# Value products of a quad of heads as one series, in the wave of its former second half

## The reference

```python
q = _split_heads(hidden_states @ q_w.T + q_b)      # hidden_states = layernorm(x), 128 rows
k = _split_heads(context @ k_w.T + k_b)            # context: 12544 rows
v = _split_heads(context @ v_w.T + v_b)
scores = jnp.einsum('bhqd,bhkd->bhqk', q, k) / jnp.sqrt(jnp.float32(HD))
scores = jnp.where(mask, -jnp.inf, scores)
probs = jax.nn.softmax(scores, axis=-1)
ctx = jnp.einsum('bhqk,bhkd->bhqd', probs, v)
x = x + ctx                                        # layers 2 and 3: ctx @ wo + bo
```

## Time and profile before

| | us |
|---|---|
| median of 3 runs | 2428.49 (2421.33 to 2435.22) |
| the profiled execution | 2424.6 |
| its span, first to last instruction | 2422.8 |
| PE busy in the span | 2268.4 |
| DVE busy | 1584.7 |
| ACT busy | 1504.9 |
| granted TensorE clock, mean | 0.958 of full |

### The profile page before, as it was taken

How to read it: one execution, slowest core, us unless ns; L and a number is a source line. 1 busy time by engine, 2 the same in 40 slices (tenths; PEclk the granted TensorE clock), 3 DMA queues, 4 the chain that set the end, 5 groups by cost and what they waited for, 6 DMA issues and landing times. The chain is left out here.

```text
span 2422.8 us, 68489 instructions
## 1 busy us (share of the span) xinstructions
PE 2268.4 (94%) x26863; PEld 1892.1 (78%) x26863; DVE 1584.7 (65%) x3621; ACT 1504.9 (62%) x3044; POOL 413.6 (17%) x353
## 2 busy tenths in 40 slices
PE   7999999988999999999877999999967999999968
PEld 6888888777788788787755888888856888888758
DVE  4777777635777777777653777777735777777532
ACT  2666666634788788887523666666633666666611
POOL 3211222002221221220002122222003222212000
PEclk7999999998999999999888999999988999999969
DMA  6677666475444344341155766666517666776345
GB/s 131 116 126 126 118 115 122 61 222 149 100 118 125 99 123 115 104 119 40 46 179 117 123 107 116 116 116 117 77 52 144 121 121 121 124 125 112 49 132 173
DMA packets 152460, 279.62 MB, mean 115 GB/s; under 512 B 32829, under 2 KB 72078, under 8 KB 152218
## 3 DMA queue, kind: packets, MB, share of 16 engines
q1 hardware_dynamic: 148842, 272.18, 54.5%
q10 hardware_dynamic: 3376, 4.03, 0.7%
HBM read 120.94 MB, written 0.33 MB: 50 GB/s over the span
## 5 line engine op out<-in xcount | busy, mean ns | idle before, releaser
L1143 DVE TENSOR_REDUCE L2x_tops<-L2x_m_bank 128x1 f32<-128x448 f32 x448 | 262.5, 618 | 130.4 <-PE L2x_m_bank L907 128.2
L1143 DVE TENSOR_REDUCE L0x_tops<-L0x_m_bank 128x1 f32<-128x448 f32 x448 | 262.5, 618 | 129.7 <-PE L0x_m_bank L907 127.4
L1143 DVE TENSOR_REDUCE L3x_tops<-L3x_m_bank 128x1 f32<-128x448 f32 x448 | 262.5, 618 | 127.6 <-PE L3x_m_bank L907 125.4
L559 DVE CUSTOM_DVE_ANT_0 L1x_p_s<-L1x_p_s,L1x_mask,L1x_neg_max 128x512 f32<-128x512 f32 (+1 forms) x400 | 288.8, 743 | 57.2 <-PE L1x_p_s L320 54.7
L452 ACT ACTIVATE L1x_prob<-L1x_p_s,L1x_neg_max 128x512 f32<-128x512 f32 (+1 forms) x400 | 274.9, 687 | 68.8 <-DVE L1x_neg_max L559 66.9
L1042 ACT ACTIVATE L3x_prob<-L3x_s_bank 128x512 f32<-128x512 f32 x448 | 219.6, 542 | 90.8 <-PE L3x_s_bank L918 89.4
L1042 ACT ACTIVATE L0x_prob<-L0x_s_bank 128x512 f32<-128x512 f32 x448 | 219.6, 542 | 90.3 <-PE L0x_s_bank L918 89.2
L1042 ACT ACTIVATE L2x_prob<-L2x_s_bank 128x512 f32<-128x512 f32 x448 | 219.6, 542 | 87.8 <-PE L2x_s_bank L918 86.5
L329 PE MATMUL L1x_p_t<-net_ident,L1x_prob 128*128 128x128 f32 x1568 | 240.5, 275 | 13.7 <-ACT L1x_probT L174 11.5
L329 PEld LDWEIGHTS L1x_p_t<-net_ident,L1x_prob 128*128 128x128 f32 x1568 | 192.7, 141 | 57.1 <-ACT L1x_probT L174 23.6
L320 PE MATMUL L1x_p_s<-L1x_k_stack,L1x_q_stack 96*128 96x512 f32 (+1 forms) x400 | 182.5, 458 | 1.9 <-DVE L1x_q_stack L542 1.9
(11 more groups left out here) (766 smaller groups left out, 4469.9 us busy)
## 6 DMA issues: line engine op xcount, KB each, us to landing
L0x_k_stack<-L0x_kT SPq DMA_DIRECT2D x333, 112.0 KB, 4.1
L2x_k_stack<-L2x_kT SPq DMA_DIRECT2D x333, 112.0 KB, 4.0
L3x_k_stack<-L3x_kT SPq DMA_DIRECT2D x333, 112.0 KB, 4.0
L1x_k_stack<-L1x_kT SPq DMA_DIRECT2D x288, 128.0 KB, 2.4
L3f_w<-in_L_ffn_w SPq DMA_DIRECT2D x16, 1024.0 KB, 7.8
L0f_w<-in_L_ffn_w SPq DMA_DIRECT2D x48, 256.0 KB, 5.2
L1x_ctx<-in_ctxT SPq DMA_DIRECT2D x24, 512.0 KB, 3.9
L0x_ctx<-in_ctxT SPq DMA_DIRECT2D x13, 896.0 KB, 6.3
```

The lines of the kernel that those rows point to most:

```text
L559: e.tensor_tensor_reduce(s, s, mask[:, odd, 0:nk], -1.0, neg_max[:, 1 - odd, h:h + 1], ALU.add, ALU.min, neg_max[:, odd, h:h + 1]).then_in ...
L1143: e.tensor_reduce(tops[:, b % 2, h, half:half + 1], m_bank[n % RING][:, 0:HALF], AX, ALU.max).then_inc(sem("m_free"), 1)
```

## The change

`values` now takes a whole quad: all seven key tiles in one series, in the wave 4q+5 in which half 1 stood. Half 0 moves there from wave 4q+3. The semaphore `valued` counts quads where it counted halves, and the three waits on it are rewritten to suit. ACT, DVE, POOL and SP keep their instructions and their order.

```diff
-            def values(k):
-                q, half = k // 2, k % 2
+            def values(q):
                 b, j = q // 4, q % 4
-                if k % 8 == 0:
+                if j == 0:
                     e.wait_ge(sem("v_made"), (b + 1) * 4)
                     if b:
                         e.wait_ge(sem("oT_copied"), b)
-                e.wait_ge(sem("s_free"), s_done(s_at(2 * k + 1, 1)))
-                for at, t in enumerate(tiles_of(half)):
+                e.wait_ge(sem("s_free"), s_done(s_at(4 * q + 3, 1)))
+                for t in range(NT):
                     for n in range(4):
                         mm = e.matmul(p_oT[32 * n:32 * n + VW, j * P:(j + 1) * P], v[:, b % 2, t, n // 2 * 8 + 2 * j + n % 2, :],
-                                      prob[:, k % 3, n, at, :], start=t == 0, stop=t == NT - 1)
+                                      prob[:, (2 * q + t // 4) % 3, n, t % 4, :], start=t == 0, stop=t == NT - 1)
                 mm.then_inc(sem("valued"), 1)
...
-                if u % 2 == 1 and 0 <= (u - 3) // 2 < NB * 8:
-                    values((u - 3) // 2)
+                if u % 4 == 1 and 0 <= (u - 5) // 4 < NB * QUADS:
+                    values((u - 5) // 4)
...
-                        e.wait_ge(sem("valued"), 8 * (b - 1))
+                        e.wait_ge(sem("valued"), 4 * (b - 1))
...
                 if k >= 3 and u % 2 == 0 and r == 0:
-                    e.wait_ge(sem("valued"), k - 2)
+                    e.wait_ge(sem("valued"), (k - 3) // 2 + 1)
...
-                e.wait_ge(sem("valued"), 8 * (b + 1))
+                e.wait_ge(sem("valued"), 4 * (b + 1))
```

## The result

The changed kernel takes 2500.21 us (median of 4 runs, 2498.92 to 2515.56); the kernel before, run beside it, 2424.91 (4 runs, 2418.02 to 2435.22). The ratio is 1.034, with a 95% interval from 1.029 to 1.039. So it is slower, as forecast, but by 75 to 82 us and not by 54.

What follows compares the result with a forecast made beforehand. PE was taken to set the pace. Each quad pays 0.88 us and gets back 0.56, so 0.32 more; 168 quads make 54 us, on 2428.5 giving 2482 us, 2.2% slower, range 2462 to 2502.

Steps and rivals of the forecast that it cites:

- Round A, 0.88 us by the slope of 0.0275: Round A: 32 more value matmuls at 0.0275 us each add 0.88 us a quad, bounds 0.85 to 0.92.
- The second maximum at 1.18, the loads' lead lost, eight scores in 0.60: Round D: second maximum waits for a reduction until 1.18 us; loads lose their lead, eight scores take 0.60, not 0.49.
- Round D's scores start at 0.78 + 0.54 = 1.32: Round D's scores wait for round C's first exponential, starting at 0.78 us and releasing them 0.54 later.
- It is before 1.32, so the exponential decides: Round D: the second maximum, at 1.18 us, precedes the scores' release at 1.32, so the exponential sets their start.
- DVE, not ACT, becomes the last: Rival: round D's scores wait for all the maxima, start near 1.43, 18 us more, 2500; shares chance 0.16.
- 0.56 us given back: Rounds C and D: without the values, round D's projection starts at 1.92 us instead of 2.48, returning 0.56 a quad.
- The same difference is taken there: Last quads of a layer, without maxima: same cost per quad; 3 us in all if two per layer got nothing back.
- the granted clock too: Profile after the change: the granted clock, like PE's busy time, stays about unchanged.
- Faster, by saved switches alone: Rival: PE takes the saved switches, nothing waits, round C shrinks to 0.59 us; 37 us less, about 2392; chance 0.04.
- No change: Rival: a wait of about 0.2 us a quad, with the loads ahead, balances the change; chance 0.04.
- Loads keeping their lead: Rival: round D's score loads are ready behind the second maximum's wait; 0.11 a quad drops out, 2464; chance 0.16.
- Slower, and more than forecast: Rival: DVE last, 2500; `k_low` late, 8 us more; or a slower series of 56, 7 us more; chance 0.16 together.

Runs made afterwards that it cites:

- Experiments 1 and 2: 12 value products of 64 columns, their result overwritten, added in round C: to the changed kernel 2492.38 us, to the kernel before 2478.45 us.
- Experiment 3: Changed kernel with DVE reducing only 224 of 448 columns of round C's first maximum: 2506.4 us, ratio 1.035 to the kernel before.
- experiment 4: Changed kernel with the first exponential of round C 128 wide instead of 384: 2505.81 us, ratio 1.034 to the kernel before.
- 2 + 5: Changed kernel with the values in two series, two tiles in round C and five in round A: 2428.65 us, ratio 1.001 to the kernel before.
- 4 + 3: The kernel before, unchanged, with four tiles of values in round C and three in round A: 2424.91 us.

## Why the prediction was right in direction and wrong in size

**What bounds the kernel: right.** PE sets the pace, and the work between its question and the answer decides. Experiments 1 and 2 show it apart from everything else.

**Round A, 0.88 us by the slope of 0.0275: right.** 0.87 measured. The series of 56 is no slower in its second half.

**The second maximum at 1.18, the loads' lead lost, eight scores in 0.60: right.** 1.18 and 0.59.

**Wrong: "Round D's scores start at 0.78 + 0.54 = 1.32", and with it "It is before 1.32, so the exponential decides".** They start at 1.42. Two things failed in that step.

- The exponential's release was taken as 0.54 behind its start: the 0.65 of a 512-wide pair, less the difference of the two mean durations. Experiment 3, where nothing else holds the scores, shows the loads going on 0.60 behind it and the matmul 0.63. The subtraction was sound: rounds C behind a 384-wide exponential go on 0.05 after its end, as round A does behind a 512-wide one. But the 0.65 was read in a round A, which has one wait ahead of its scores, and was used for round D, which has two; there the loads go on 0.11 after the end, and the matmul 0.03 behind them.
- The second maximum was called not deciding because it comes before 1.32. But it and eight scores still stand ahead of the projection, and experiment 4, with the exponential out of the way, has the projection at 1.98 all the same, not at 1.92. So even with the release as forecast, DVE would have decided. That is nearly the rival "DVE, not ACT, becomes the last" (scores at 1.43, 18 us more); it should not have stood as a rival, but as a second term, with the later of the two taken.

The term "0.56 us given back" thus measured 0.47, and the net 0.32 a quad 0.40: 0.08 x 168 = 13 us. With it the sum is 67 where the forecast had 54. That is the quad of the steady part; over whole layers at like clock the traces come to some 55 us up to the last maxima, less than 0.40 a quad, since the first quads of a layer got partly faster and some quads of the kernel before took up to 1.1 us longer than their like.

**The layers' ends and the clock: put at too little.** "The same difference is taken there" gave under 1 us a layer. The ends are 1.7 us longer where both have the full clock and 3.8 where both have much less. The prediction had "the granted clock too" among what stays unchanged, and this is the second thing it had wrong: the lower clock took 10 to 16 us in the ends and, by the last blocks of layers 2 and 3, another 3.1 + 8.1 = 11. Against it stand the 5.4 us of layer 0's start and the 7.0 us outside the layers. These are figures of one execution of each kernel. Why the clock falls in more places is not shown.

**The rivals.** Faster, by saved switches alone: the switches are really saved, as the shorter six scores show (0.28 instead of 0.38), but only into a wait. No change: nothing balanced. Loads keeping their lead: they lost it. Slower, and more than forecast: of its three conditions DVE came nearly true, the other two not at all (`k_low` is done at 1.71, the projection starts at 2.01, and 32 more values cost 0.87). The rule of "TensorEngine Tiling (Array Packing)" in the Trainium skill (key properties), that a change of tiling mode drains TensorE, isn't contradicted: the entry that was saved did free time on PE. No run turned it into a shorter kernel, because the freed time ended in a wait.

**The range.** 2462 to 2502 had its upper end at the DVE case alone. The changed kernel's median of 2500.21 lies just inside; measured as a ratio on the base of 2428.49 it is 2511, outside. That the plain median falls inside is luck: the kernel before took 3.6 us less beside it than in the base of the forecast. The ends and the clock would have had to be added to the DVE case.

## What to carry to other kernels

Before taking work away from between a question and its answer (here scores and maxima that wait on a ring of three banks), find how long the answer takes and keep that much other work there; here two tiles of seven, 0.57 us, were enough, and one, 0.35 us, was not, and the splits 2 + 5 and 4 + 3 take the same time. Where an engine meets two waits in a row, work out both to the point where the series behind them ends and take the later one: the profile puts the idle time down to the one that is met first, and shortening one alone can show nothing. When a release time is read in one round and used in another, compare the waits ahead of the two: here a second wait went with 0.06 us more until the load and 0.09 until the matmul.

## What the runs showed of the hardware

- The same 24 narrow matmuls a quad cost nothing in a wait (2492.38 against 2500.21 us) and 54 us where PE is the bound.
- PE's loads went on 0.05 us after the end of an exponential, 384 or 512 wide, where one wait stands ahead of them, and 0.11 us after it, 128 or 384 wide, where two stand there, the second as an instruction of 51 ns.
- The granted clock fell to 0.61 to 0.69 over layer ends in which PE was busy for some 76% of the time, and to 0.60 over 8 us in which it was busy for all of them. With the same instructions it was 0.79, 0.79 and 1.00 in the three ends of one execution.
- A series of 56 values took 3.13 us where the granted clock was 0.53, and 1.74 us where it was 1.00.
